# Order tables of a fused cross-attention and sparse-FFN kernel: gather a step later, two products in halves, the first scores ahead of the first values

## The chip, the cores and the metric

One NeuronCore of one Trainium2 chip runs the whole program in one launch. The number looked at is the device time of one execution in microseconds (us). Before the change it is 963.16 us, the median of three runs between 959.63 and 963.48 us.

## What is computed

Eight batches of 512 queries by 256 features attend to 1024 context rows with 16 heads of 16 features; then a router picks 128 of the 512 rows of each batch, these go through causal self-attention and a gated FFN, and are put back:

```
q, k, v = LN(x) @ Wq.T, ctx @ Wk.T, ctx @ Wv.T          # 16 heads of 16
x = x + softmax(q k.T / 4, masked keys off) v @ Wo.T
y = LN(x)
idx = top_k(y @ w_router, 128);  x_sel = y[idx]          # the 128 best rows
h = rmsnorm(x_sel, g1);  att = causal_attention(h @ Wqkv.T) @ Wout.T
h2 = rmsnorm(x_sel + att, g2)
x_ff = silu(h2 @ W1.T) * (h2 @ W2.T) @ W3.T              # 682 wide
out = x + y, with idx rows replaced: x[idx] + x_sel + att + x_ff
```

All data are float32. The weights' layout is prepared on the host.

## The kernel before, in words

The program is written engine by engine: each of TensorE (PE), VectorE (DVE), ScalarE (ACT), GpSimd (POOL) and SyncE (SP, which issues the DMAs) has its list of instructions, in an order written out by hand, and they meet in semaphores. Nothing is scheduled by a planner.

After a prologue, an outer loop goes over the eight batches, here called passes 0 to 7, and each pass has 32 steps: 4 head groups by 8 key tiles of 128. In step s, PE issues

- the *scores* of step s (`pe_scores`, L436): four products of 32x128 keys by 32x512 queries into two of three PSUM bank pairs, once ACT has freed both. ACT turns them into `probs` with two Exp instructions of 128x1024 (L466), each of which frees its pair;
- the *values* of step s-1 (`pe_values`, L455): `probs` by `va` into `o_bank`, once ACT's second Exp of that step is done. At the first tile of a head group (steps 1, 9, 17, 25, where s-1 is a multiple of 8) they wait for `o_free` too: `dve_norm` (L544, stages norm0 to norm3) has to have read the group before out of `o_bank`;
- a *filler*: one stage of other work, as the table `PE_SLOT` says, with the step as its number. All fillers of the loop write one PSUM bank, `m_bank` (`MISC`), and take it when ACT or DVE has evicted the filler before (`take_bank`, `bank_free`).

A step with no filler is called empty below. The fillers are of two kinds. "P" is projection for the next batch: keys `K00` to `K11`, values `V0` to `V3`, the transposes `xT0`, `xT1` of the normalised input, queries `Q0`, `Q1`. "F" is the output projection and the FFN of the batch before: `wo0`, `wo1`, `spread` (router scores onto all partitions), then on DVE `rank0` to `rank3`, which end in the selection matrix `sel`, then `gather` (`sel` by `y`), `selT`, `hidT`, `kq`, `v`, `fs` (FFN attention scores), `pv`, `wout`, `hid2T`, `u0`, `w0`, `u1`, `w1`, `down` (the last product, by W3), `scat1`, `scat0`. Pass 0 has no "F" and, in the table `PE_SLOT_0`, the rest of batch 0's own projections ("I"); pass 7 has no "P". `ACT_SLOT` and `DVE_ORDER` say in which order ACT and DVE evict.

In the prologue PE runs 18 products of no use (`spare_products`, L257), then K00, the transposes, K01 and Q0 of batch 0; then it transposes the table of valid keys (`valid`, L988), which DVE copies, and computes V0, which DVE multiplies by it. Only then does the loop begin. After pass 7 a tail runs the FFN of batch 7 with nothing beside it but more products of no use.

Of the kernel before, what the change touches and what calls it, by code (L numbers as in the profile page):

```python
# [5 lines left out]
P = 128  # L6
# [3 lines left out]
D = 256  # L10
# [4 lines left out]
KC = D // P  # L15
# [12 lines left out]
FT = 6  # L28
# [14 lines left out]
MISC = 7  # L43

BANK_FIRST = {"xT0": 0, "xT1": 1, "K00": 2, "Q0": 3, "K01": 4, "valid": 5, "V0": 7}
# [11 lines left out]
           ("F", "fs", FS_STEP, False), ("P", "Q0", 16, False), ("P", "V2", 17, False), ("P", "Q1", 18, False),  # L57
# [3 lines left out]
ACT_SLOT = [("P", "K00", 0), ("P", "K01", 1), ("P", "K10", 5), ("F", "spread", 6), ("P", "K11", 7), ("P", "xT0", 8),  # L61
            ("P", "xT1", 9), ("F", "selT", 11), ("F", "hidT", 12), ("F", "v", 15), ("F", "fs", FS_STEP), ("P", "differ", 21),
            ("F", "hid2T", 23), ("F", "u0", 24), ("F", "u1", 26)]
DVE_ORDER = [("A", "norm3"), ("F", "wo0"), ("F", "wo1"), ("P", "V0"), ("F", "y"), ("P", "stats"), ("P", "xn"), ("F", "rank0"),
# [4 lines left out]

PE_SLOT_0 = [("I", "V1", 0, False), ("I", "K10", 1, False), ("I", "V2", 2, False), ("I", "K11", 3, False),  # L70
# [4 lines left out]
ACT_SLOT_0 = [("I", "K10", 1), ("I", "K11", 3), ("P", "K00", 8), ("P", "K01", 9), ("P", "K10", 10), ("P", "K11", 11),  # L75
              ("P", "xT0", 15), ("P", "xT1", 17), ("P", "differ", 20)]
DVE_ORDER_0 = [("I", "V1"), ("I", "V2"), ("I", "V3"), ("I", "Q1"), ("P", "stats"), ("N", "norm0"), ("P", "xn"), ("P", "V0"),
# [12 lines left out]
SPARE_FIRST = 18  # L90

# [8 lines left out]
def program(nc, io, out):  # L100
    with ExitStack() as top:
# [163 lines left out]
        def pe_project(pe, stage, i):  # L265
# [32 lines left out]
        def pe_ffn(pe, stage, i):  # L298
# [73 lines left out]
            elif stage == "down":  # L372
                pe.wait_ge(gate_ready, 2)
                pe.sem_inc(gate_ready, -2)
                dst = take_bank(pe, i)
                product(dst[:, 0:D], [(gate[:, f], w3[:, f]) for f in range(FT)]).then_inc(done["down"], 1)
# [412 lines left out]
        with ExitStack() as ctx:  # L789
# [129 lines left out]
            def _(dve):  # L919
# [19 lines left out]
                dve_project(dve, "V0", 0, BANK_FIRST["V0"], valid[:, 0])  # L939
# [42 lines left out]
            def _(pe):  # L982
                def valid_keys():
                    pe.wait_ge(consts, 1)
# [343 lines left out]
```

## Time and profile before

| | |
|---|---|
| median of 3 runs | 963.16 us (959.63 to 963.48) |
| profiled execution, its time | 963.8 us |
| its span, first to last instruction | 962.0 us |
| granted TensorE clock, mean | 0.993 |
| PE busy | 896.8 us (93%) |
| ACT busy | 575.0 us (60%) |
| DVE busy | 340.8 us (35%) |
| POOL busy | 79.0 us (8%) |
| 16 DMA engines | 34 GB/s on average |

In the chain of time the passes look like this in the trace: the first scores start at 23.78 us, pass 1 at about 124 us, pass 3 runs from 345.09 to 456.84 us, pass 7 from 789.90 us, and the tail from about 888 us to the end. The busy time of an engine counts an instruction from start to modelled end; where two overlap they count once. A time is read below mostly from start to start: between the start of one group and that of the next lies all that the first costs, its wait for the next included.

### The profile page before, as it was taken

What the parts mean: (1) busy time and instruction counts of PE and PEld (TensorE: products, weight loads), DVE (VectorE), ACT (ScalarE), POOL (GpSimd) and SP (SyncE); (2) the same over time, 40 slices, a digit from 0 to 9 for tenths busy, and PEclk for the clock granted to TensorE, in tenths of its full rate; (3) what the DMA queues carried; (4) which work ended last, traced back from release to release, by engine and by line L of the source; (5) the groups of instructions that cost most, each with busy time, mean ns of one, the idle gap of its engine ahead of it and who ended that gap; (6) DMA issues with size and microseconds to landing.
All of it is one profiled execution on the core that took longest, in us unless ns stands there. A gap on an engine that the chain in (4) does not pass through costs nothing. (4 is left out here: it accounts for less than half of the span.)

```text
span 962.0 us, 25188 instructions
## 1 busy us (share of the span) xinstructions
PE 896.8 (93%) x10277; PEld 338.6 (35%) x10277; DVE 340.8 (35%) x886; ACT 575.0 (60%) x653; POOL 79.0 (8%) x130
## 2 busy tenths in 40 slices
PE   6999999999999999999999999999989999899874
PEld 2323232333333432334323433334323332334434
DVE  2222136232543227331453316342273315321631
ACT  2567766666666666665576766666666767676010
POOL 4000100010100101000000101011001100010010
PEclk9999999999999999999999999999999999999998
DMA  5150200020010200020010200002000000000000
GB/s 170 42 184 1 72 3 23 24 73 24 5 42 2 73 23 23 23 68 15 16 39 8 73 23 24 24 3 72 24 1 24 29 24 1 24 2 24 1 1 25
DMA packets 23789, 32.47 MB, mean 34 GB/s; under 512 B 1102, under 2 KB 20856, under 8 KB 23672
## 3 DMA queue, kind: packets, MB, share of 16 engines
q1 hardware_dynamic: 23672, 30.81, 9.9%
q8 instruction: 85, 1.39, 0.6%
q14 instruction: 32, 0.26, 0.1%
HBM read 26.61 MB, written 4.19 MB: 32 GB/s over the span
## 5 line engine op out<-in xcount | busy, mean ns | idle before, releaser
L466 ACT ACTIVATE probs<-pair_bank 128x1024 f32<-128x1024 f32 x512 | 496.3, 1021 | 270.6 <-ACTq L465 270.6
L436 PE MATMUL pair_bank<-q_sb,k_sb 32*128 32x512 f32 x2048 | 292.1, 639 | 13.9 <-PEq L434 13.9
L455 PE MATMUL o_bank<-probs,va 128*32 128x512 f32 x2048 | 272.7, 604 | 6.3 <-PEq L449 5.2
L436 PEld LDWEIGHTS pair_bank<-q_sb,k_sb 32*128 32x128 f32 x2048 | 81.3, 183 | 140.0 <-issue 140.0
L455 PEld LDWEIGHTS o_bank<-probs,va 128*32 128x32 f32 x2048 | 41.3, 108 | 197.2 <-issue 110.9
L252 PE MATMUL m_bank<-wv_sb,ctx_in 128*32 128x256 f32 x1024 | 62.8, 386 | 0.6 <-PEq L262 0.6
L544 DVE STREAM_TRANSPOSE o_blk<-o_bank 128x512 f32<-128x512 f32 x32 | 22.9, 717 | 110.5 <-DVEq L543 110.5
L252 PE MATMUL m_bank<-ctx_in,wk_sb 128*32 128x512 f32 x480 | 57.0, 592 | 0.0
L585 DVE TENSOR_SCALAR va<-m_bank,valid 128x256 f32<-128x256 f32 x64 | 28.0, 479 | 80.8 <-DVEq L579 80.8
L252 PEld LDWEIGHTS m_bank<-hid_t,w 128*32 128x32 f32 x1440 | 41.3, 111 | 19.5 <-issue 19.4
L252 PE MATMUL m_bank<-hid_t,w 128*32 128x128 f32 x1440 | 46.0, 275 | 2.2 <-PEq L262 1.7
L252 PEld LDWEIGHTS m_bank<-wv_sb,ctx_in 128*32 128x32 f32 x1024 | 33.8, 111 | 36.7 <-issue 21.1
L597 DVE TENSOR_SCALAR q_sb<-m_bank,parity 128x512 f32<-128x512 f32 x30 | 21.1, 747 | 34.3 <-DVEq L595 34.3
L474 ACT ACTIVATE k_sb<-m_bank 128x512 f32<-128x512 f32 x30 | 17.9, 597 | 24.2 <-ACTq L473 24.2
L614 DVE TENSOR_TENSOR x<-x,m_bank 128x512 f32<-128x512 f32 x14 | 9.6, 688 | 61.7 <-DVEq L613 61.7
L257 PE MATMUL o_bank<-before 128*128 128x512 bf16 x118 | 28.8, 402 | 2.7 <-POOL before L846 2.7
L754 POOL TENSOR_TENSOR mask_in<-mask_in,mask_row 128x256 int32<-128x256 int32 x32 | 23.3, 760 | 78.8 <-POOLq L751 78.8
L252 PE MATMUL m_bank<-xn_t,wq_sb 128*32 128x512 f32 x240 | 28.6, 595 | 0.0
L252 PEld LDWEIGHTS m_bank<-ctx_in,wk_sb 128*32 128x32 f32 x480 | 15.6, 110 | 35.9 <-issue 35.9
L769 POOL TENSOR_SCALAR_AFFINE_SELECT p_f<-p_f 128x2048 f32<-128x2048 f32 x8 | 16.1, 2006 | 141.9 <-POOLq L767 141.9
L762 POOL TENSOR_SCALAR veps<-mv 128x4 f32<-128x4 f32 x8 | 1.9, 233 | 311.0 <-POOLq L761 311.0
L252 PE MATMUL m_bank<-wo,o_t 128*32 128x256 f32 x448 | 26.7, 379 | 0.0
(168 smaller groups left out, 647.0 us busy)
## 6 DMA issues: line engine op xcount, KB each, us to landing
ctx_in<-in_ctxT SPq DMA_DIRECT2D x8, 1024.0 KB, 7.3
x_in<-in_x SPq DMA_DIRECT2D x8, 512.0 KB, 3.9
x<-in_x SPq DMA_DIRECT2D x8, 512.0 KB, 3.7
mask_in<-in_mask SPq DMA_DIRECT2D x8, 512.0 KB, 3.9
out_dram<-out_sb SPq DMA_DIRECT2D x8, 512.0 KB, 2.8
mask_row<-in_mask SPq DMA_DIRECT2D x8, 128.0 KB, 5.4
wqkv<-in_wqkvT SPq DMA_DIRECT2D x1, 768.0 KB
w<-in_w1T SPq DMA_DIRECT2D x1, 682.0 KB
```

What stands on the lines that cost most here:

```text
L252: last = nc.tensor.matmul(dst[j], a[:, j], c, start=(n == 0), stop=(n == len(pairs) - 1))
L257: last = nc.tensor.matmul(dst, before[:, 0, 0:P], before[:, 1], start=True, stop=True)
L436: last = nc.tensor.matmul(pair_bank[pairs[r // 2]][:, r % 2], key_tile(b, s, r), query_tile(b, s, r), start=True, stop=True)
L455: last = nc.tensor.matmul(o_bank[32 * r:32 * r + 32], va[b % 2][:, t, HV * h:HV * h + 32], probs[s % 2][:, r], start=(t == 0), stop=(t == ...
L466: nc.scalar.activation(probs[s % 2][:, 2 * e:2 * e + 2, :], pair_bank[p][:], ACT.Exp, scale=HD ** -0.5).then_inc(s_free[p], 1)
L474: nc.scalar.activation(k_sb[b % 2][:, m, half * 512:(half + 1) * 512], bank[i], ACT.Copy).then_inc(bank_free[i], 1)
L544: nc.vector.transpose(o_blk[:], o_bank[:]).then_inc(o_free, 1)
L585: last = nc.vector.tensor_scalar(by_head(va[b % 2][:, t])[:, :, 0:HD], bank[i][:, e * D:(e + 1) * D].rearrange("p (h d) -> p h d", h=H), o ...
L597: last = nc.vector.tensor_scalar(q_sb[b % 2][:, m, par], bank[i], parity[:, par:par + 1], None, ALU.mult)
L614: nc.vector.tensor_tensor(x1[:, 2 * pr:2 * pr + 2], x1[:, 2 * pr:2 * pr + 2], bank[i].rearrange("p (t d) -> p t d", t=2), ALU.add).then_in ...
L754: last = nc.gpsimd.tensor_tensor(mask_words[:, t * WORDS:(t + 1) * WORDS], mask_words[:, t * WORDS:(t + 1) * WORDS], first, ALU.subtract)
L769: nc.gpsimd.affine_select(out=flat, in_=flat, compare_op=ALU.is_ge, fill=0.0, base=0, pattern=[[0, H], [1, CAP]], channel_multiplier=-1).t ...
```

## The change

It is one edit of tables, with what they need:

- `gather` and its followers `selT`, `hidT` go from steps 10, 11, 12 to 11, 12, 13; `kq` and what comes later stay. `V1`, which stood at step 13, goes to 17, `V2` from 17 to 18, `Q1` from 18 to 20, `V3` from 20 to the empty step 22.
- `K11`, the fourth piece of keys, is computed in two halves (`K11:0`, `K11:1`) in steps 7 and 8; `xT0`, `xT1` go from 8, 9 to 9, 10.
- `down` is computed in two halves in steps 28 and 29; `scat1`, `scat0` go from 29, 30 to 30, 31. Step 31 was empty.
- Batch 0's `valid` and `V0` leave the prologue for step 0 of pass 0, after scores(0), and use `m_bank`; the other "I" stages go one step later. In their place 10 products of no use stand after Q0, and the semaphore `spare_done`, which GpSimd waits for before it finishes the constant `before`, moves behind them.

A half of a product takes the bank only in its first part and signals only after its second. The tail keeps `down` whole.

```diff
-           ("P", "V0", 4, True), ("P", "K10", 5, False), ("F", "spread", 6, False), ("P", "K11", 7, False),
-           ("P", "xT0", 8, False), ("P", "xT1", 9, False), ("F", "gather", 10, False), ("F", "selT", 11, False),
...
+           ("P", "V0", 4, True), ("P", "K10", 5, False), ("F", "spread", 6, False), ("P", "K11:0", 7, False), ("P", "K11:1", 8, False),
+           ("P", "xT0", 9, False), ("P", "xT1", 10, False), ("F", "gather", 11, False), ("F", "selT", 12, False),
...
-             ("F", "rank1"), ("N", "norm0"), ("F", "rank2"), ("F", "rank3"), ("F", "gather"), ("F", "base"), ("P", "V1"),
-             ("F", "kq"), ("N", "norm1"), ("P", "Q0"), ("P", "V2"), ("P", "Q1"), ("F", "pv"), ("P", "V3"), ("F", "wout"),
+             ("F", "rank1"), ("N", "norm0"), ("F", "rank2"), ("F", "rank3"), ("F", "gather"), ("F", "base"),
+             ("F", "kq"), ("N", "norm1"), ("P", "Q0"), ("P", "V1"), ("P", "V2"), ("F", "pv"), ("P", "Q1"), ("F", "wout"),
...
+        def share(part, n):
+
+            return range(n) if part is None else range(part * n // 2, (part + 1) * n // 2)
...
-                dst = take_bank(pe, i)
-                product(dst, [(wk[:, c, m * P:(m + 1) * P], ctx_in[:, c, half * 512:(half + 1) * 512]) for c in range(KC)]
-                        ).then_inc(done["K"], 1)
+                dst = bank[i] if part == 1 else take_bank(pe, i)
+                last = product(dst, [(wk[:, c, m * P:(m + 1) * P], ctx_in[:, c, half * 512:(half + 1) * 512])
+                                     for c in share(part, KC)], part != 1, part != 0)
+                if part != 0:
+                    last.then_inc(done["K"], 1)
...
-                spare_products(SPARE_FIRST, o_bank[:]).then_inc(spare_done, 1)
+                spare_products(SPARE_FIRST, o_bank[:])
...
-                valid_keys()
-                pe.wait_ge(w_in["wv"], 16)
-                pe_project(pe, "V0", BANK_FIRST["V0"])
+                spare_products(SPARE_Q0, o_bank[:]).then_inc(spare_done, 1)
```

The next two blocks are PE's order in pass 2 from `spread` (step 6) to `selT`, before and then after; L436 and L449 are the scores, L455 and L468 the values.

```order
204 L243 MATMUL m_bank<-ident,score 128x128 x4
205 L436 MATMUL pair_bank<-q_sb,k_sb 128x512 x4
206 L455 MATMUL o_bank<-probs,va 32x512 x4
207 L252 MATMUL m_bank<-ctx_in,wk_sb 32x512 x8
208 L436 MATMUL pair_bank<-q_sb,k_sb 128x512 x4
209 L455 MATMUL o_bank<-probs,va 32x512 x4
210 L243 MATMUL m_bank<-ident,xn 128x128 x4
...
216 L252 MATMUL m_bank<-y,sel 32x256 x16
```

```order
207 L245 MATMUL m_bank<-ident,score 128x128 x4
208 L449 MATMUL pair_bank<-q_sb,k_sb 128x512 x4
209 L468 MATMUL o_bank<-probs,va 32x512 x4
210 L254 MATMUL m_bank<-ctx_in,wk_sb 32x512 x4
211 L449 MATMUL pair_bank<-q_sb,k_sb 128x512 x4
212 L468 MATMUL o_bank<-probs,va 32x512 x4
213 L254 MATMUL m_bank<-ctx_in,wk_sb 32x512 x4
214 L449 MATMUL pair_bank<-q_sb,k_sb 128x512 x4
215 L468 MATMUL o_bank<-probs,va 32x512 x4
216 L245 MATMUL m_bank<-ident,xn 128x128 x4
...
222 L254 MATMUL m_bank<-y,sel 32x256 x16
```

Between `spread` and the gather (`y,sel`) there are now five pairs of scores and values instead of four, and the same filler work; half of the keys' product lies one step later. In the last steps of the same pass, `down` and what follows it on PE stood and stand so:

```order
270 L252 MATMUL m_bank<-w,gate 32x256 x24
271 L436 MATMUL pair_bank<-q_sb,k_sb 128x512 x4
272 L455 MATMUL o_bank<-probs,va 32x512 x4
273 L252 MATMUL m_bank<-att,sel_t 32x256 x8
...
276 L252 MATMUL m_bank<-att,sel_t 32x256 x8
277 L436 MATMUL pair_bank<-q_sb,k_sb 128x512 x4
278 L455 MATMUL o_bank<-probs,va 32x512 x4
279 L436 MATMUL pair_bank<-q_sb,k_sb 128x512 x4
```

```order
274 L254 MATMUL m_bank<-w,gate 32x256 x12
275 L449 MATMUL pair_bank<-q_sb,k_sb 128x512 x4
276 L468 MATMUL o_bank<-probs,va 32x512 x4
277 L254 MATMUL m_bank<-w,gate 32x256 x12
...
283 L254 MATMUL m_bank<-att,sel_t 32x256 x8
284 L449 MATMUL pair_bank<-q_sb,k_sb 128x512 x4
285 L468 MATMUL o_bank<-probs,va 32x512 x4
286 L254 MATMUL m_bank<-ctx_in,wk_sb 32x512 x8
```

Two values followed by scores with nothing between them (rows 278, 279) are the empty step 31; it is now filled. At the program's start PE's order was and is:

```order
5 L252 MATMUL pair_bank<-xn_t,wq_sb 32x512 x8
6 L988 MATMUL pair_bank<-ident,rows 128x64
7 L252 MATMUL m_bank<-wv_sb,ctx_in 32x256 x16
8 L436 MATMUL pair_bank<-q_sb,k_sb 128x512 x4
9 L252 MATMUL m_bank<-wv_sb,ctx_in 32x256 x16
```

```order
5 L254 MATMUL pair_bank<-xn_t,wq_sb 32x512 x8
6 L264 MATMUL o_bank<-before 128x512 x10
7 L449 MATMUL pair_bank<-q_sb,k_sb 128x512 x4
8 L1003 MATMUL m_bank<-ident,rows 128x64
9 L254 MATMUL m_bank<-wv_sb,ctx_in 32x256 x16
10 L449 MATMUL pair_bank<-q_sb,k_sb 128x512 x4
```

The first scores now stand ahead of the transpose of the valid keys (`rows`) and of V0 (`wv_sb,ctx_in`).

## Rows read from the trace of the kernel before

**Rows 1.** Windows: length; busy us (instructions) of PE, PEld, DVE, ACT, POOL; clock; DMA.

```profile
20.00:40.00 20.00, 19.16 (x197) 6.98 (x201) 3.50 (x16) 8.95 (x10) 0.63 (x1) 0.91 0.01 2
345.09:456.84 111.75, 107.43 (x1268) 40.27 (x1269) 42.42 (x109) 71.34 (x82) 9.03 (x13) 1.00 0.10 31
```

**Rows 2.** Waits of PE: us in total, times, longest.

```profile
PE pair_bank L436 <- PEq L434: 13.9, 40, 1.3
```

**Rows 3.** Timeline of pass 3, PE, steps 7 to 10: start, us, instructions [idle before].

```profile
372.44 1.90 PE L252 MATMUL m_bank<-ctx_in,wk_sb 128*32 128x512 f32 x16
374.27 1.14 PE L436 MATMUL pair_bank<-q_sb,k_sb 32*128 32x512 f32 x8
...
376.93 1.14 PE L436 MATMUL pair_bank<-q_sb,k_sb 32*128 32x512 f32 x8
378.85 1.06 PE L455 MATMUL o_bank<-probs,va 128*32 128x512 f32 x8 [0.79 <-PEq L449]
...
381.50 1.06 PE L455 MATMUL o_bank<-probs,va 128*32 128x512 f32 x8
383.98 1.93 PE L252 MATMUL m_bank<-y,sel 128*32 128x256 f32 x32 [1.41 <-PEq L262]
```

**Rows 4.** The same stretch, DVE: norm0's first read, and the last `sel`.

```profile
378.03 0.72 DVE L544 STREAM_TRANSPOSE o_blk<-o_bank 128x512 f32<-128x512 f32 x1 [0.19 <-DVEq L543]
...
383.36 0.29 DVE L647 TENSOR_SCALAR sel<-iota_r,rank 128x128 f32<-128x128 f32 x1
```

**Rows 5.** Timeline of pass 3, PE, steps 20 to 23.

```profile
419.30 1.91 PE L252 MATMUL m_bank<-wv_sb,ctx_in 128*32 128x256 f32 x32
421.14 1.14 PE L436 MATMUL pair_bank<-q_sb,k_sb 32*128 32x512 f32 x8
422.21 1.06 PE L455 MATMUL o_bank<-probs,va 128*32 128x512 f32 x8
423.10 1.05 PE L252 MATMUL m_bank<-wout,os_t 128*32 128x256 f32 x16
424.07 1.14 PE L436 MATMUL pair_bank<-q_sb,k_sb 32*128 32x512 f32 x8
...
426.74 1.14 PE L436 MATMUL pair_bank<-q_sb,k_sb 32*128 32x512 f32 x8 [0.53 <-PEq L434]
```

**Rows 6.** Timeline, PE: scores of pass 3's step 31 and of pass 4's step 0.

```profile
454.41 1.14 PE L436 MATMUL pair_bank<-q_sb,k_sb 32*128 32x512 f32 x8
...
456.84 1.14 PE L436 MATMUL pair_bank<-q_sb,k_sb 32*128 32x512 f32 x8 [0.30 <-PEq L434]
```

**Rows 7.** Timeline, PE: pass 7, scores of step 10 and its gather.

```profile
817.46 1.14 PE L436 MATMUL pair_bank<-q_sb,k_sb 32*128 32x512 f32 x8 [0.24 <-PEq L434]
821.27 1.93 PE L252 MATMUL m_bank<-y,sel 128*32 128x256 f32 x32 [1.68 <-PEq L262]
```

**Rows 8.** Timeline of the start: Q0 and its eviction, valid keys, V0, first scores.

```profile
15.62 1.90 PE L252 MATMUL pair_bank<-xn_t,wq_sb 128*32 128x512 f32 x16
...
17.70 1.41 DVE L597 TENSOR_SCALAR q_sb<-pair_bank,parity 128x512 f32<-128x512 f32 x2 [5.97 <-DVEq L595]
...
20.28 0.24 PE L988 MATMUL pair_bank<-ident,rows 64*128 64x64 f32 x1 [2.77 <-PEq L262]
...
20.45 3.39 PE L252 MATMUL m_bank<-wv_sb,ctx_in 128*32 128x256 f32 x32
20.56 0.23 DVE L936 COPY valid<-pair_bank 128x64 f32<-128x64 f32 x1 [0.53 <-PE pair_bank L988]
...
23.78 1.31 PE L436 MATMUL pair_bank<-q_sb,k_sb 32*128 32x512 f32 x8
```

**Rows 9.** Timeline, PE: V1 after the eviction of V0; scores(8) of pass 0.

```profile
25.65 1.93 PE L252 MATMUL m_bank<-wv_sb,ctx_in 128*32 128x256 f32 x32 [0.56 <-PEq L262]
...
51.31 1.14 PE L436 MATMUL pair_bank<-q_sb,k_sb 32*128 32x512 f32 x8 [0.29 <-PEq L434]
```

**Rows 10.** Timeline, PE: twelve products of no use at the tail's start.

```profile
888.83 2.76 PE L257 MATMUL pair_bank<-before 128*128 128x512 bf16 x12
```

More of the change, by code:

```diff
@@ L43 @@
 MISC = 7
-BANK_FIRST = {"xT0": 0, "xT1": 1, "K00": 2, "Q0": 3, "K01": 4, "valid": 5, "V0": 7}
+BANK_FIRST = {"xT0": 0, "xT1": 1, "K00": 2, "Q0": 3, "K01": 4, "valid": MISC}
 BANK_LAST = {"wo0": 0, "wo1": 1, "spread": 7, "gather": 0, "selT": 1, "hidT": 7, "kq": 0, "v": 1, "pv": 7, "wout": 0,
@@ L53 @@
 PE_SLOT = [("P", "K00", 0, False), ("P", "K01", 1, False), ("F", "wo0", 2, False), ("F", "wo1", 3, False),
[3 rows of a table removed]
-           ("F", "fs", FS_STEP, False), ("P", "Q0", 16, False), ("P", "V2", 17, False), ("P", "Q1", 18, False),
[1 row of a table removed]
[3 rows of a table added]
+           ("F", "fs", FS_STEP, False), ("P", "Q0", 16, False), ("P", "V1", 17, False), ("P", "V2", 18, False),
+           ("F", "pv", 19, False), ("P", "Q1", 20, False), ("F", "wout", 21, False), ("P", "V3", 22, False),
+           ("F", "hid2T", 23, False),
            ("F", "u0", 24, False), ("F", "w0", 25, False), ("F", "u1", 26, False), ("F", "w1", 27, False),
[1 row of a table removed]
-ACT_SLOT = [("P", "K00", 0), ("P", "K01", 1), ("P", "K10", 5), ("F", "spread", 6), ("P", "K11", 7), ("P", "xT0", 8),
-            ("P", "xT1", 9), ("F", "selT", 11), ("F", "hidT", 12), ("F", "v", 15), ("F", "fs", FS_STEP), ("P", "differ", 21),
+           ("F", "down:0", 28, False), ("F", "down:1", 29, False), ("F", "scat1", 30, False), ("F", "scat0", 31, False)]
+ACT_SLOT = [("P", "K00", 0), ("P", "K01", 1), ("P", "K10", 5), ("F", "spread", 6), ("P", "K11", 8), ("P", "xT0", 9),
+            ("P", "xT1", 10), ("F", "selT", 12), ("F", "hidT", 13), ("F", "v", 15), ("F", "fs", FS_STEP), ("P", "differ", 21),
             ("F", "hid2T", 23), ("F", "u0", 24), ("F", "u1", 26)]
 DVE_ORDER = [("A", "norm3"), ("F", "wo0"), ("F", "wo1"), ("P", "V0"), ("F", "y"), ("P", "stats"), ("P", "xn"), ("F", "rank0"),
[3 rows of a table removed]
[3 rows of a table added]
              ("F", "scat0")]
-PE_SLOT_0 = [("I", "V1", 0, False), ("I", "K10", 1, False), ("I", "V2", 2, False), ("I", "K11", 3, False),
[1 row of a table removed]
+PE_SLOT_0 = [("I", "valid", 0, False), ("I", "V0", 0, False), ("I", "V1", 1, False), ("I", "K10", 2, False),
[1 row of a table added]
              ("P", "K10", 10, False), ("P", "K11", 11, False), ("P", "V0", 12, False), ("P", "V1", 13, False),
@@ L74 @@
              ("P", "V3", 21, False), ("P", "Q1", 23, False)]
-ACT_SLOT_0 = [("I", "K10", 1), ("I", "K11", 3), ("P", "K00", 8), ("P", "K01", 9), ("P", "K10", 10), ("P", "K11", 11),
+ACT_SLOT_0 = [("I", "K10", 2), ("I", "K11", 4), ("P", "K00", 8), ("P", "K01", 9), ("P", "K10", 10), ("P", "K11", 11),
               ("P", "xT0", 15), ("P", "xT1", 17), ("P", "differ", 20)]
-DVE_ORDER_0 = [("I", "V1"), ("I", "V2"), ("I", "V3"), ("I", "Q1"), ("P", "stats"), ("N", "norm0"), ("P", "xn"), ("P", "V0"),
+DVE_ORDER_0 = [("I", "V0"), ("I", "V1"), ("I", "V2"), ("I", "V3"), ("I", "Q1"), ("P", "stats"), ("N", "norm0"), ("P", "xn"), ("P", "V0"),
                ("P", "V1"), ("N", "norm1"), ("P", "V2"), ("P", "Q0"), ("P", "V3"), ("P", "Q1"), ("N", "norm2")]
@@ L246, in program, with product @@
         strips = [slice(j, j + 32) for j in range(0, P, 32)]
-        def product(dst, pairs):
+        def product(dst, pairs, begins=True, ends=True):
             for n, (a, c) in enumerate(pairs):
                 for j in strips:
-                    last = nc.tensor.matmul(dst[j], a[:, j], c, start=(n == 0), stop=(n == len(pairs) - 1))
-            return last
+                    last = nc.tensor.matmul(dst[j], a[:, j], c, start=(begins and n == 0),
+                                            stop=(ends and n == len(pairs) - 1))
+            return last
+        def share(part, n):
+            return range(n) if part is None else range(part * n // 2, (part + 1) * n // 2)
         def spare_products(n, dst):
@@ L372, in pe_ffn @@
             elif stage == "down":
[L373 to L376, printed above, removed]
+                if part != 1:
+                    pe.wait_ge(gate_ready, 2)
+                    pe.sem_inc(gate_ready, -2)
+                dst = bank[i] if part == 1 else take_bank(pe, i)
+                last = product(dst[:, 0:D], [(gate[:, f], w3[:, f]) for f in share(part, FT)], part != 1, part != 0)
+                if part != 0:
+                    last.then_inc(done["down"], 1)
             elif stage in ("scat1", "scat0"):
@@ L1020, in _ @@
                         for stage, at, early, kind in todo:
-                            if at == s and not early and kind in ("P", "I"):
-                                pe_project(pe, stage, MISC)
+                            if at == s and stage == "valid":
+                                valid_keys()
+                            elif at == s and not early and kind in ("P", "I"):
+                                pe_project(pe, *stage_part(stage))
                             elif at == s and not early and stage == "fs":
```

16 lines of the change are left out of this document (9 added, 7 removed), and 8 rows, old and new, of tables (DVE_ORDER, PE_SLOT, PE_SLOT_0).

## The prediction, made before the changed kernel was run

> **What bounds the kernel now.** I read the window of a middle pass first [rows 1]: in pass 3 PE is busy 107.43 of 111.75 us, at a granted clock of 1.00, ACT 71.34 and DVE 42.42. The reader is to see that PE's list of products sets the time, so that the change, which removes no product, can only win where PE waits, some 4 us a pass. Then the waits of PE [rows 2] name the commonest one: scores that wait for ACT (L434), 40 times, 13.9 us. Last the timeline of PE in one pass for the places, with DVE beside it for what ends them [rows 3 to 6].
>
> I count from start to start. In a step whose filler is full size, scores take 1.07 us (421.14 to 422.21) and values 0.89 (422.21 to 423.10) [rows 5], 1.95 together, and the filler's own time comes on top. An empty step should take 1.95 and takes 2.43 (454.41 to 456.84) [rows 6], because the next scores need a pair of banks that ACT has still to read. So an empty step wastes 0.48 us, and any filler over that size hides ACT.
>
> **Gather a step later, keys in halves.** Before, values(9) start at 381.50 and the gather could start 0.89 later, at 382.39; it starts at 383.98, 1.59 later [rows 3], since the last `sel` ends at 383.65 [rows 4]. There is a second wait above it: scores(9) start at 376.93, values(8) could start 1.07 later, at 378.00, and start at 378.85, 0.85 later [rows 3]. These values open a head group and need `o_bank` read by norm0, whose transpose runs from 378.03 to 378.75 [rows 4]; it stands on DVE behind rank1. DVE's chain up to norm0 starts from `spread` in step 6, ahead of everything moved, so I take 378.85 as fixed.
>
> A half product costs more than half. A filler of 16 instructions (wout) takes 0.97 (423.10 to 424.07), one of 32 of the same shape (V3) 1.84 (419.30 to 421.14) [rows 5]: two small ones are 0.10 more than one large one, the price of a boundary. K11 takes 1.83 (372.44 to 374.27) [rows 3], a half so 0.97. After the change: K11:0 at 372.44, scores(8) 373.41, K11:1 at 375.36, scores(9) 376.33, values(8) wanted at 377.40. They wait for norm0 until 378.85, 1.45 us: 0.60 more than before, with the boundary hidden in the wait. From there the times are as before through scores(10) at 380.43 and values(9) at 381.50; then xT1 (0.69, as xT0 has it between values(8) and scores(10): 380.43 - 378.85 - 0.89) instead of the gather, scores(11) at 383.08, the gather at 385.03. `sel` has been ready for 1.4 us. So 1.59 goes, 0.60 comes back at norm0 and 0.10 of work is added: **0.9 us a pass**. What is late next is norm0; the cover of the gather is 1.4 us.
>
> `hidT` and `kq` now stand in neighbouring steps. `hid` follows the gather through DVE and POOL as before and moves with it, so `hidT` waits for nothing new. `kq` waits for ACT's eviction of `hidT`, with 1.95 us of scores and values between; I take nothing. V1, V2 and Q1 only change places; K11's eviction moves with its second half, and POOL's list is the same in the loop.
>
> **Step 22.** It was empty and followed a step in which ACT also squares the mask: scores(22) at 424.07, scores(23) at 426.74 [rows 5], 2.67 for 1.95. With V3 there, **0.7 us a pass** go. V3's eviction comes two steps later, hence `ctx_free`, on which SP queues the next context load, a store behind it. The context is wanted at step 0 of the next pass, ten steps of some 3.5 us later: hidden. The store and the loads behind it in SP's queue slip a step at most and are needed steps later.
>
> **Step 31.** `down` in halves and scat1, scat0 a step later fill it: 0.48 less 0.10 for the boundary, **0.38 a pass**, in pass 7 too.
>
> **Pass 7** has no "P". Scores(10) start at 817.46, the gather at 821.27 [rows 7]: 3.81 for 1.95, so 1.86 waits. After, step 10 is empty in place of step 13, at 2.43 both, and the gather, at 821.84, comes 0.9 after the `sel` that it waited for. With step 31 2.24.
>
> **The start.** Q0 ends about 17.46, DVE evicts it until 19.11; PE idles to 20.28, transposes the valid keys, and V0 takes 3.33 until the scores at 23.78 [rows 8], where V1 costs 1.93 busy [rows 9]; the granted clock of that stretch is 0.91 against 1.00 [rows 1]. V0, right behind the idle time, ran at the lower of the two levels (1.2 GHz), and that cost 1.5 us. After: ten products of no use, 0.23 each at full clock (2.76 for 12 [rows 10]), to 19.76, past Q0's eviction; scores(0) 19.76, valid at 20.83. V0 now shares `m_bank` with it and waits for DVE's copy: 0.51 from transpose to end of the copy [rows 8], and 0.3 for the way back, the gap between `sel` and the gather [rows 3, 4]. V0 21.64, scores(1) 23.48. Values(0) wait for V0's eviction: V1 waited for it before, from V0's end at 23.78 to 25.65, 1.87 [rows 8, 9]. So values(0) at 25.35, 0.8 late, V1 at 26.24, scores(2) 28.08, then five full steps (K10, V2, K11, V3, Q1) of 3.79 and the empty step 7: scores(8) at 49.5 against 51.31 [rows 9]. **1.8 us**, net of the added products.
>
> On that clock there is a rule in the Trainium skill (TensorE: Matmul & The Clock Gate, Part 1: The HAM clock gate): the array runs at half rate by default and is released by activity, and idling throttles it again. The trace agrees where PE idled 2.77 us ahead of V0 and V0 took 3.39. By that rule the ten products keep the clock up. The page also says (Part 2, single matmul latency) that a lone product cannot hide its drain while a stream can, which speaks against halves: an estimate from its 166 ns at the high clock would charge 13 added boundaries 2.2 us. The 0.10 of the rows decides, of which seven count, 0.7 us.
>
> **Sum.** Six passes (1 to 6) at 0.9 + 0.72 + 0.38 = 2.0 are 12.0; pass 7 2.2; the start 1.8: 16.0 us. The tail is untouched. The profiled execution took 963.8 us with 1.8 outside its span; it stands 0.6 above the median. So 947.8 on its own scale, about **947 us** on the median's.
>
> **Bounds of what the trace does not show.** The start: if the ten products and the first steps run at the low level, they take twice 0.23 each and V0 3.33, which costs 3.8 and turns 1.8 into -2.0; if values(0) wait for nothing, it is +2.6. I take 1.8, nearest to the rows at full clock. Gather: between 0.3 (the 1.59 taken back by norm0 and by `kq` behind `hidT`) and 1.5 (norm0 no later relative to the values); 0.9 is worked from a time that I hold fixed. A boundary: from nothing to twice 0.10; step 22: 0.5 to 0.7. Together a gain of 6 x 1.1 + 1.5 - 2.0 = 6 us at the low end and 6 x 2.7 + 2.4 + 2.6 = 21 at the high end, 957 and 942. Passes also differ by up to 1 us with the same work; these need not stay.
>
> **Rivals.**
> 1. *The start gives nothing back.* The clock falls in spite of the ten products, or V0, now between scores and values, delays both. For: two new waits within 5 us of the loop's begin (0.8 for the bank, 0.8 for V0's eviction). Against: each is shorter than the 2.77 that came before the low clock. Start at -2.0: 950.8 us.
> 2. *The gather's wait moves rather than goes.* Norm0 stands in DVE's list between rank1 and rank2 and PE now comes to values(8) sooner. If the wait there takes all that the gather's gave up, 5.4 us are missing: 952.4 us. For: 0.85 us of it is there already. Against: norm0's start hangs on DVE's chain, which PE's order after `spread` doesn't touch.
> 3. *One bank for all fillers becomes the bound*, and the time is higher than before. With every step filled, each filler waits for the eviction of the one before, with 1.95 us of cover. Q0's eviction ends 1.65 after its product and 0.2 to 0.3 more brings the bank back [rows 8]; Q1 now stands ahead of wout, and `hidT` ahead of `kq`. Cover is nearly used up for Q1. To be slower by 0.5%, 20.8 us must be lost at the 13 such places (seven times `hidT` to `kq`, six times Q1 to wout), 1.6 us each; at 1.7 us the time is 969 us. Against: in the trace Q1 stands in step 18 ahead of pv, and pv shows no wait.
> 4. *The change doesn't do what it says*: the freed steps meet stalls of another kind (DVE or ACT late for one step), and only the empty steps 22 and 31 give, 7 us: 956 us.
>
> **How the numbers follow.** My forecast has 0.60, rival 1 0.17, rival 2 0.13, rival 4 0.06, rival 3 0.04. What a measurement can tell from no change is 0.5%, 4.8 us, so faster is below 958.3. Forecast and rivals 1 and 2 are faster, rival 4 mostly (0.04 of 0.06): 0.94 faster, 0.02 within, 0.04 slower. The range, 942.5 to 954 us, takes in the forecast's own and rivals 1 and 2.
>
> **What would show it.** Right: in passes 1 to 6 no wait ahead of the gather, 1.4 to 1.5 us ahead of values(8), no empty step from 0 to 31, a pass in 108.6 to 109.5 us; scores(0) near 19.8 us, V0 in about 1.9 us, scores(8) of pass 0 near 49.5; pass 7 without a wait at its gather. Wrong: a wait at the gather or at `kq`, one at wout behind Q1's eviction, V0 at 3.3 us, or halves that cost more than 0.97 and 1.41 us.

## The result and the profile after

The changed kernel takes 946.38 us, the median of four runs (944.77 to 948.13), against 962.21 us (959.63 to 963.48, four runs) for the kernel before beside it: a ratio of 0.984, 95% interval 0.981 to 0.987. A second series gave 946.38 us again (0.984, 0.982 to 0.985). That is 15.8 us; the forecast was 16.0, 947 us. So close a match is luck: the start was off by 3.0 us one way, and passes 1 to 6 by 2.1 and the tail, whose code the change leaves alone, by 0.6 the other way. The experiments are mostly about the first two.

The profiled execution took 947.94 us with a span of 946.2, against 963.8 and 962.0. Cut at scores(0) of passes 1 and 7 and at the tail's first product of no use, the two traces compare so:

| stretch | before, us | after, us | gained | forecast |
|---|---|---|---|---|
| start to scores(0) of pass 1 | 123.62 | 124.86 | -1.24 | 1.8 |
| passes 1 to 6 | 666.28 | 652.14 | 14.14 | 12.0 |
| pass 7 | 98.93 | 96.60 | 2.33 | 2.2 |
| tail, to the end of the span | 73.17 | 72.6 | 0.6 | 0 |

This is PE in pass 3 of the changed kernel, steps 7 to 11, from the timeline (start, us, instructions, idle before); L449 are the scores, L468 the values, and it answers to [rows 3].

```profile
369.28 1.04 PE L254 MATMUL m_bank<-ctx_in,wk_sb 128*32 128x512 f32 x8
370.25 1.14 PE L449 MATMUL pair_bank<-q_sb,k_sb 32*128 32x512 f32 x8
...
372.21 1.04 PE L254 MATMUL m_bank<-ctx_in,wk_sb 128*32 128x512 f32 x8
373.18 1.14 PE L449 MATMUL pair_bank<-q_sb,k_sb 32*128 32x512 f32 x8
376.03 1.07 PE L468 MATMUL o_bank<-probs,va 128*32 128x512 f32 x8 [1.71 <-issue]
...
381.33 1.06 PE L468 MATMUL o_bank<-probs,va 128*32 128x512 f32 x8
382.22 1.91 PE L254 MATMUL m_bank<-y,sel 128*32 128x256 f32 x32
```

And DVE beside it, answering to [rows 4]: norm0's transpose and the last `sel`.

```profile
375.21 0.72 DVE L557 STREAM_TRANSPOSE o_blk<-o_bank 128x512 f32<-128x512 f32 x1 [0.54 <-DVEq L556]
...
380.53 0.29 DVE L660 TENSOR_SCALAR sel<-iota_r,rank 128x128 f32<-128x128 f32 x1
```

A half product takes 0.97 (369.28 to 370.25), as forecast. The gather follows its values after 0.89 with no wait, 1.4 us after `sel` (380.82). The wait sits ahead of values(8) now, and ends with norm0's transpose (375.93). The profile calls its cause "issue", but the time fits DVE's end to 0.1 us. Here it is 1.71, in passes 5 and 6 1.62 and 1.68; in passes 1, 2 and 4 it is 1.37. Why norm0 comes later in three of the passes no run shows. Step 22 and the end of the pass, answering to [rows 5, 6]:

```profile
418.50 1.14 PE L449 MATMUL pair_bank<-q_sb,k_sb 32*128 32x512 f32 x8
...
420.45 1.91 PE L254 MATMUL m_bank<-wv_sb,ctx_in 128*32 128x256 f32 x32
422.29 1.14 PE L449 MATMUL pair_bank<-q_sb,k_sb 32*128 32x512 f32 x8
...
440.18 1.48 PE L254 MATMUL m_bank<-w,gate 128*32 128x256 f32 x24
441.59 1.14 PE L449 MATMUL pair_bank<-q_sb,k_sb 32*128 32x512 f32 x8
```

V3 ends where the next scores start, without a wait, and half of `down` takes 1.41. The window of the whole pass, with the columns of [rows 1]:

```profile
341.94:450.81 108.87, 106.86 (x1272) 40.19 (x1268) 41.91 (x109) 71.29 (x82) 8.85 (x13) 1.00 0.10 32
```

Pass 3 went from 111.75 to 108.87 us, PE's busy time hardly: what went is idle time. The start is another matter. PE, DVE and POOL there, answering to [rows 8, 9] (L264 are the products of no use):

```profile
17.70 2.11 PE L264 MATMUL o_bank<-before 128*128 128x512 bf16 x9 [0.16 <-issue]
...
19.90 1.14 PE L449 MATMUL pair_bank<-q_sb,k_sb 32*128 32x512 f32 x8
...
21.65 1.93 PE L254 MATMUL m_bank<-wv_sb,ctx_in 128*32 128x256 f32 x32 [0.41 <-PEq L269]
...
22.73 2.79 POOL L767 TENSOR_TENSOR mask_in<-mask_in,mask_row 128x256 int32<-128x256 int32 x4 [0.28 <-POOLq L764]
23.51 1.14 PE L449 MATMUL pair_bank<-q_sb,k_sb 32*128 32x512 f32 x8
23.75 2.04 DVE L595 COPY va<-valid 128x16 f32<-128x16 f32 x8 [2.25 <-DVEq L592]
...
25.70 0.86 DVE L598 TENSOR_SCALAR va<-m_bank,valid 128x256 f32<-128x256 f32 x2
26.76 1.55 PE L468 MATMUL o_bank<-probs,va 128*32 128x512 f32 x8 [2.11 <-PEq L465]
28.01 3.23 PE L254 MATMUL m_bank<-wv_sb,ctx_in 128*32 128x256 f32 x32
31.17 1.14 PE L449 MATMUL pair_bank<-q_sb,k_sb 32*128 32x512 f32 x8
```

Up to scores(1) all is as worked out: scores(0) 19.90 (19.76), V0 21.65 (21.64) at the full clock, scores(1) 23.51 (23.48). Then the eight copies of the valid column take DVE 2.04 us, not 0.7, values(0) start at 26.76 instead of 25.35, and behind 2.11 us without work the clock is at its lower level: V1 takes 3.23. The granted clock says the same (0.91 over the window below; 0.50 of 2.4 GHz in the part from 28 to 30 us, 1.00 from 32 us on):

```profile
20.00:40.00 20.00, 17.48 (x181) 7.01 (x185) 4.79 (x15) 8.35 (x9) 5.24 (x9) 0.91 0.01 2
```

Scores(2) were forecast for 28.08 and start at 31.17, 3.1 later, and that is the whole miss of the start: scores(8) at 52.55 against 49.5 forecast.

### The profile page after: what moved, and what is told of

Its sections match the earlier page's. It is cut to its first block and busy times, and to the rows that moved or that the text cites. A ratio compares the mean times of both kernels' runs of the same rounds, so it can differ in the third digit from the quotient of the medians.

```text
span 946.2 us, 25202 instructions
## 1 busy us (share of the span) xinstructions
PE 895.5 (95%) x10280; PEld 338.3 (36%) x10287; DVE 339.9 (36%) x886; ACT 574.7 (61%) x653; POOL 78.1 (8%) x130
## 3 DMA queue, kind: packets, MB, share of 16 engines
q8 instruction: 85, 1.39, 0.6%
## 5 line engine op out<-in xcount | busy, mean ns | idle before, releaser
L449 PE MATMUL pair_bank<-q_sb,k_sb 32*128 32x512 f32 x2048 | 292.1, 639 | 8.8 <-PEq L447 8.7
L468 PE MATMUL o_bank<-probs,va 128*32 128x512 f32 x2048 | 273.2, 605 | 11.5 <-issue 9.1
L449 PEld LDWEIGHTS pair_bank<-q_sb,k_sb 32*128 32x128 f32 x2048 | 81.0, 183 | 131.1 <-issue 131.1
L468 PEld LDWEIGHTS o_bank<-probs,va 128*32 128x32 f32 x2048 | 41.3, 108 | 202.0 <-issue 117.7
L264 PE MATMUL o_bank<-before 128*128 128x512 bf16 x122 | 31.4, 413 | 3.3 <-POOL before L859 2.7
L653 DVE SCALAR_TENSOR_TENSOR ties<-all_scores,score,before 128x512 f32<-128x512 f32 x32 | 24.1, 752 | 6.6 <-DVEq L652 4.8
```

The costliest lines, as they stand in the source:

```text
L264: last = nc.tensor.matmul(dst, before[:, 0, 0:P], before[:, 1], start=True, stop=True)
L449: last = nc.tensor.matmul(pair_bank[pairs[r // 2]][:, r % 2], key_tile(b, s, r), query_tile(b, s, r), start=True, stop=True)
L468: last = nc.tensor.matmul(o_bank[32 * r:32 * r + 32], va[b % 2][:, t, HV * h:HV * h + 32], probs[s % 2][:, r], start=(t == 0), stop=(t == ...
L653: nc.vector.scalar_tensor_tensor(out=ties[t % 2][:], in0=all_scores[:], scalar=score[:, t:t + 1], in1=before[:, t], op0=ALU.is_equal, op1= ...
```

## The experiments

All start from the changed kernel but e11. Times are medians, each with its ratio to the kernel before beside it. "Scores(8)" is their start in pass 0 in the profiled execution; in the changed kernel it is 52.55 us, in the kernel before 51.31. The runs come from several series, and the median of the kernel before moved between 960.8 and 962.4 us from one to the next; a difference of medians from different series is good to about 1.5 us, and the stretches of the traces tell more.

| kernel | us | ratio (95%) | scores(8) |
|---|---|---|---|
| changed, two series | 946.38, 946.38 | 0.984 (0.981 to 0.987), 0.984 (0.982 to 0.985) | 52.55, 52.57 |
| e1, old start | 944.4 | 0.983 (0.981 to 0.985) | 50.32 |
| e2, own tile | 943.95 | 0.981 (0.980 to 0.983) | 49.70 |
| e3, copies first | 944.02 | 0.981 (0.980 to 0.983) | 48.82 |
| e4, gap filled | 945.82 | 0.984 (0.981 to 0.986) | 50.97 |
| e10, e2 without the ten | 946.81 | 0.984 (0.982 to 0.987) | 50.83 |
| e5, K11 whole | 946.63 | 0.985 (0.983 to 0.987) | |
| e6, norm0 first | 942.07 | 0.981 (0.979 to 0.983) | |
| e7, down whole | 948.88 | 0.988 (0.986 to 0.989) | |
| e8, old middle | 956.27 | 0.996 (0.994 to 0.997) | |
| e9, e2 + e3 + e6 | 939.77 | 0.976 (0.974 to 0.978) | |
| e11, before, mask sooner | 959.5 | 0.997 (0.995 to 0.999) | |

**e1, the start as before.**

```diff
-                spare_products(SPARE_Q0, o_bank[:]).then_inc(spare_done, 1)
+                valid_keys()
+                pe_project(pe, "V0", BANK_FIRST["V0"])
```

(with `PE_SLOT_0`, `ACT_SLOT_0`, `DVE_ORDER_0`, the banks and `spare_done` as in the kernel before)

> The changed kernel with the start of the kernel before: valid keys and V0 in the prologue, no ten products, the other stages of batch 0 a step earlier again. The traces put scores(8) of pass 0 at 51.31 us before and at 52.55 after, so my theory now is that the new start costs 1.2 us: this kernel is 1.2 us faster than the profiled execution of the changed one, about 946.7 on the profiled scale (947.9 there), with the passes unchanged at 108.4 to 108.9 us. The rival, my prediction's own sum, says that the new start is worth 1.8 us and its loss was a disturbance of one execution: then this kernel takes 1.8 us more than an undisturbed run of the changed one (944.8), 946.6, and scores(8) lies at 51.3 in both cases. What tells them apart is the changed kernel's other runs, two at 944.8 and two at 948: the start may be worth 1.8 in some and cost 1.2 in others.

Measured: 944.4 us, scores(8) at 50.32. The new start costs time, 2.2 us between the two traces and about 2 between the medians, though those intervals overlap. It is more than the expected 1.2, because in this execution the old start itself was quicker than in the kernel before: PE waited 2.21 us for the valid keys, not 2.77, and V0 took 2.95, not 3.39. The first has a cause in the traces: DVE's conversion of the valid keys' table (`rows`), ahead of PE's transpose, began at 19.25 in both and took 0.23 instead of 0.78, with GpSimd's mask differences beside it in both. The prediction's 1.8 us of gain is refuted.

**e2, GpSimd as early as before.** The ten products read a tile of their own, and `spare_done` stands again behind the first 18.

```diff
+        spare = sb("spare", [P, S], BF16)
...
-                spare_products(SPARE_FIRST, o_bank[:])
+                spare_products(SPARE_FIRST, o_bank[:]).then_inc(spare_done, 1)
...
-                spare_products(SPARE_Q0, o_bank[:]).then_inc(spare_done, 1)
+                own_spares(SPARE_Q0, o_bank[:])
```

> The changed kernel, but the ten products after Q0 read a tile of their own, so spare_done is signalled after the first 18 products as in the kernel before and GpSimd finishes `before` and does batch 0's mask differences (L767) some 4.9 us earlier. Theory (GpSimd in DVE's way): the eight copies of the valid column ahead of V0's eviction took 2.04 us instead of 0.74 because GpSimd's mask differences ran beside them (22.73 to 25.5 us); moved to about 17.9 to 20.6 us they are gone: copies 0.7, values(0) at 25.4 instead of 26.76, the clock stays at the high level, V1 takes 1.93 instead of 3.23, scores(8) of pass 0 at 49.5, every run near 943.5 to 944.5. Rival (the copies were slow for another reason, such as reading `valid` just written): copies still 2.0 us, scores(8) at 52.5 in a run with the low clock, runs at 944.8 to 948.

Measured: 943.95 us, and the timeline of its start:

```profile
17.89 2.77 POOL L773 TENSOR_TENSOR mask_in<-mask_in,mask_row 128x256 int32<-128x256 int32 x4 [3.73 <-POOLq L770]
...
23.92 0.72 DVE L601 COPY va<-valid 128x16 f32<-128x16 f32 x8 [2.25 <-DVEq L598]
...
25.60 1.06 PE L474 MATMUL o_bank<-probs,va 128*32 128x512 f32 x8 [0.78 <-PEq L471]
26.46 1.94 PE L255 MATMUL m_bank<-wv_sb,ctx_in 128*32 128x256 f32 x32
```

DVE's list is the same; only GpSimd's place in time is another, and the copies take 0.72 instead of 2.04. Values(0) wait 0.78, as the prediction had it (0.8), and no product of the start runs at the low level. The theory holds, its numbers too (49.70 against 49.5). The page SBUF — State Buffer of the Trainium skill says (its term "shared port pair") that VectorE and GpSimd arbitrate for one pair of ports with an exclusive lock; these two traces agree in that the copies take longer beside GpSimd, 2.04 against 0.72 us. DVE's eviction from PSUM, begun at 25.70 when GpSimd ended (25.52), took its usual 0.86, so they say nothing of evictions beside GpSimd.

**e3, copies ahead of the wait.**

```diff
-                dve.wait_ge(done["V"], 1)
-                dve.sem_inc(done["V"], -1)
+                if n == 0 and b == 0:
+                    copies()
+                dve.wait_ge(done["V"], 1)
+                dve.sem_inc(done["V"], -1)
```

> The changed kernel, but for batch 0 DVE makes the eight copies of the valid column before it waits for V0 instead of after. If the chain from V0 to values(0) is what stalls PE, the copies run from about 21.6 us beside V0, before GpSimd's mask differences begin at 22.7, and V0's eviction is 0.87 us from 23.8: values(0) at about 24.8 instead of 26.76, no low clock, scores(8) of pass 0 at about 48.9 us, runs at 943 to 944. If GpSimd still comes in DVE's way, the eviction waits for it to end (25.5) and values(0) stay near 26.7.

Measured: 944.02 us, values(0) at 24.73, scores(8) at 48.82, the earliest of all. The copies, begun at 21.55, were slow again, 1.87 us, with GpSimd at `before` until 22.1 and at the mask from 22.63, but PE no longer waited for them. One detail is against my expectation of a blocked eviction: it ran from 23.66 to 24.54 beside GpSimd's mask differences in 0.88, its usual time. In this execution what reads PSUM was not held up; the copies within SBUF were.

**e4, the wait filled with work of no use.**

```diff
+                        if b == 0 and s == 1:
+                            own_spares(8, o_bank[:])
```

> The changed kernel with eight more products of no use (0.23 us each) in the wait ahead of values(0), step 1 of pass 0, on a tile of their own. It takes the low clock apart from the wait: theory (the 2.11 us of idle PE let the clock fall, and the low level cost 1.7 us): values(0) still at about 26.8, but V1 1.93 instead of 3.23 and values(0) 1.07 instead of 1.55, scores(8) of pass 0 at 50.9 instead of 52.55, runs at 946.3 or less and less spread than 944.8 to 948.1. Rival (the clock falls whatever PE does there): V1 at 3.2 us again, scores(8) at 52.5.

```profile
24.71 1.90 PE L270 MATMUL o_bank<-spare 128*128 128x512 bf16 x8
...
26.87 1.07 PE L474 MATMUL o_bank<-probs,va 128*32 128x512 f32 x8 [0.27 <-PEq L471]
27.73 1.94 PE L255 MATMUL m_bank<-wv_sb,ctx_in 128*32 128x256 f32 x32
```

Values(0) come as late (26.87), yet V1 takes 1.94, scores(2) follow values(0) after 2.73 us instead of 4.41, and scores(8) start 1.6 us sooner. So of the 3.1 us missed at the start 1.4 are the copies and 1.7 the clock behind the wait. In the medians this is within the noise (945.82 against 946.38), and the runs spread as before, 944.63 to 948.95. The runs of this program differ for another reason too: the two profiled executions of the changed kernel, 1.56 us apart, both have the low clock there (V1 at 3.23 and 3.60) and scores(8) at 52.55 and 52.57; they part in the tail, 72.6 against 71.1 us. The low clock came in five of the six profiled executions that had this 2.1 us wait; in e8's it did not, with nothing else changed in pass 0.

**e10, e2 without the ten products.** The line `own_spares(SPARE_Q0, o_bank[:])` is gone.

> The kernel with the ten products on their own tile (943.95 us), without those ten products; GpSimd is as early as there. Theory (the ten products are there for the clock): PE idles some 1.9 us behind Q0, scores(0) start about 0.5 us sooner, at 19.4, and the clock may fall behind it: V0 or V1 at 3 us as in the old start, 1.0 to 1.5 us lost, 944.5 to 945. Rival (an idle stretch under 2 us doesn't bring the low clock): no product at the low level, scores(8) of pass 0 at 49.2, 943.5 us, and the ten products are worth nothing.

```profile
19.84 1.14 PE L455 MATMUL pair_bank<-q_sb,k_sb 32*128 32x512 f32 x8 [2.36 <-PEq L453]
...
21.68 3.19 PE L255 MATMUL m_bank<-wv_sb,ctx_in 128*32 128x256 f32 x32 [0.41 <-PEq L275]
```

V0 runs at the low level. Scores(0) win nothing, against the 0.5 us expected: here as in e2 they start 4.26 us after Q0 does (Q0 itself is 0.23 sooner), so the ten products cost no time. Scores(8) are 1.13 us later than in e2 (1.36 counted from Q0), which is what those products are worth here. The median is 2.9 us higher; of the 2.1 us between the two profiled executions another 1.3 lies in pass 7, whose code is the same (97.68 against 96.37 us), where the low level came behind a wait of 1.28 us ahead of scores(17) in e10 and not in e2. The Trainium skill's rule that the prediction cited (TensorE: Matmul & The Clock Gate, Part 1: The HAM clock gate) fits e2, e4 and e10: idle ahead, low level behind. It does not tell e8 from the five others.

**e5, K11 whole in step 7, step 8 empty.**

```diff
-("P", "K11:0", 7, False), ("P", "K11:1", 8, False),
+("P", "K11", 7, False),
```

> The changed kernel with K11 whole in step 7 and step 8 empty; all else as changed. By the prediction's working values(8) wait for norm0 at a time that PE doesn't move, so the halves gain nothing there: the empty step's 0.48 us is taken out of the wait, which shrinks from 1.4 to about 1.1 us, a pass stays at 108.4 to 108.9 us and the time within 0.5 us of the changed kernel. Rival (a filled step is worth its 0.48 here too, less 0.10 for the boundary): 0.38 a pass, 2.3 us slower.

Measured: 946.63 us, passes 1 to 6 in 652.80 us against 652.14, 0.1 a pass. The wait ahead of values(8) fell from 1.37 to 1.00. The halves of K11 gain next to nothing: norm0 sets the time at that place.

**e6, norm0 ahead of rank1 on DVE.**

```diff
-             ("F", "rank1"), ("N", "norm0"), ("F", "rank2"), ...
+             ("N", "norm0"), ("F", "rank1"), ("F", "rank2"), ...
```

> The changed kernel with norm0 ahead of rank1 in DVE's order. Theory: the 1.4 to 1.7 us that values(8) wait in each of the six passes end because norm0's transpose starts about 2 us sooner, right behind rank0; the last sel stays where it is, and so the gather, 1.4 us ahead of its need until now, would wait about 0.1 to 0.4 us. A gain of 1.0 to 1.4 us a pass, 6 to 8 us in all. Rival (PE has no use for the earlier values since the next link, the end of the rank chain, is as late): the wait moves to the gather in full and nothing is gained.

Values(8) and the gather of pass 3 in its timeline:

```profile
372.25 1.06 PE L468 MATMUL o_bank<-probs,va 128*32 128x512 f32 x8
...
378.81 1.93 PE L254 MATMUL m_bank<-y,sel 128*32 128x256 f32 x32 [0.18 <-PEq L269]
```

942.07 us; passes 1 to 6 take 645.56 us, 6.6 less or 1.10 a pass, and the gather waits 0.18 to 0.49 there. Pass 7 pays: its gather waits 0.87, which it did not before, and the pass takes 1.06 us more, 97.66. The expectation had 6 to 8 us in all and left that out; the traces say 5.5 for the seven passes, the medians 4.3. What the change left at values(8) was real idle time, and one swap collects most of it.

**e7, down whole in step 28.**

```diff
-("F", "down:0", 28, False), ("F", "down:1", 29, False), ("F", "scat1", 30, False), ("F", "scat0", 31, False)]
+("F", "down", 28, False), ("F", "scat1", 29, False), ("F", "scat0", 30, False)]
```

> The changed kernel with down whole in step 28, the scatters in 29 and 30, step 31 empty again. Theory: seven passes pay 0.48 for the empty step and save 0.10 for the boundary: 0.38 each, 2.7 us slower than the changed kernel. Rival (halves cost more than 0.10, up to what a drained pipeline would cost, 0.17 each, or hide something else): between 1.5 and 4 us slower.

948.88 us, 2.5 slower; passes 1 to 6 take 654.37 us, 0.37 a pass more, and pass 7 0.84. A boundary is 0.1 us, not the 0.17 of the rival.

**e8, the middle of a pass as before.**

```diff
-("P", "K11:0", 7, False), ("P", "K11:1", 8, False), ("P", "xT0", 9, False), ("P", "xT1", 10, False), ("F", "gather", 11, False), ...
+("P", "K11", 7, False), ("P", "xT0", 8, False), ("P", "xT1", 9, False), ("F", "gather", 10, False), ..., ("P", "V1", 13, False), ...
```

> The changed kernel with the middle of a pass as before: K11 whole in step 7, the transposes in 8 and 9, gather, selT, hidT in 10, 11, 12, V1 in 13; V2 in 17, Q1 in 20, V3 in 22, and step 18 empty. Theory: in passes 1 to 6 the wait at the gather is back (1.6 from start to start for 0.6 less at norm0, 0.1 less for the boundary) and step 18 wastes 0.48: 1.4 us a pass, 8.3 in six, and 1.9 in pass 7: 10.2 us slower than the changed kernel. Rival (the gather's place is worth little, the gain came from passes that had stalls in the kernel before): only the 0.48 of step 18 in six passes and little more, 3 us.

956.27 us, 9.9 slower. Passes 1 to 6 take 660.90 us, 8.8 more (8.3 expected), pass 7 98.46, 1.9 more. The waits are back to the digit in passes 1 and 2: 0.78 ahead of values(8) and 1.40 at the gather; the others have up to 0.35 more at one of the two. The gather's place, with the step that it fills, is well over half of the whole gain; the two are not taken apart, and the empty step (18 here) is 0.48 a pass of it by the sum.

**e9, three edits together.** e2, e3 and e6.

> The changed kernel with three of the edits tried before together: norm0 ahead of rank1, the ten products on a tile of their own (so GpSimd works as early as in the kernel before), the eight copies for batch 0 ahead of the wait for V0. If the edits add up: 942.07 of norm0 first, less the 2.4 us by which either start edit beat the changed kernel, less up to 0.8 us because values(0) wait for nothing: 939 to 940 us. Rival (the start edits and norm0 first share a gain, or the time won at the start is lost again in pass 0, which has empty steps): no better than 941.

939.77 us, a ratio of 0.976 to the kernel before (0.974 to 0.978), the fastest of all. Its 6.6 us against the changed kernel are what the parts promise.

**e11, the kernel before with the mask squared in step 20.** One entry of `ACT_SLOT`:

```diff
-("F", "fs", FS_STEP), ("P", "differ", 21),
+("F", "fs", FS_STEP), ("P", "differ", 20),
```

> The kernel before (not the changed one) with one entry changed: ACT squares the mask (`differ`) in step 20 instead of 21, so the next mask is loaded and GpSimd takes its differences (L754) one step, 3.8 us, sooner. The passes gained 2.1 us more than the prediction's sum, and in the kernel before GpSimd's differences overlap norm2's multiplication on DVE (L549) in passes 2 to 5, where that took 0.68 to 0.99 us instead of 0.42, and w0 waited up to 1.0 us; in the changed kernel they don't overlap. Theory (that collision is the 2.1 us): all L549 at 0.42, no wait at w0 in passes 1 to 6, 2.0 us gained; and as ACT now squares beside a full step, the wait ahead of scores(23) falls from 0.53 to 0.30, 1.4 us more: 3.4 us faster than the kernel before. Rival (the waits at w0 have another cause): they stay, and only the 1.4 us are gained.

To read it, first pass 3 of the kernel before, timeline of POOL, DVE and PE in steps 24 and 25 (L754 are the mask differences, L549 norm2's multiplication, L252 at 435.69 is w0):

```profile
431.85 2.98 POOL L754 TENSOR_TENSOR mask_in<-mask_in,mask_row 128x256 int32<-128x256 int32 x4 [4.95 <-POOLq L751]
...
432.62 0.93 DVE L549 TENSOR_TENSOR o_nrm<-o_blk,inv_all 128x256 f32<-128x256 f32 x1
...
435.69 1.52 PE L252 MATMUL m_bank<-hid_t,w 128*32 128x128 f32 x48 [1.00 <-PEq L262]
```

The same place in the changed kernel, DVE:

```profile
428.18 0.43 DVE L562 TENSOR_TENSOR o_nrm<-o_blk,inv_all 128x256 f32<-128x256 f32 x1
```

And in e11, POOL:

```profile
427.12 2.79 POOL L754 TENSOR_TENSOR mask_in<-mask_in,mask_row 128x256 int32<-128x256 int32 x4 [1.17 <-POOLq L751]
```

with L549 at 431.44 in 0.43 us. In e11 no pass has a wait at w0, all L549 take 0.42 or 0.43, and scores(23) wait 0.30 instead of 0.53. 959.5 us against 962.38 is a gain of 2.9 (1.3 to 4.8 by the interval), 3.4 expected; the interval takes in the rival's 1.4 too. In its trace passes 1 to 6 take 662.42 us (785.98 less 123.56) against 666.28, so 3.9 less: 1.4 is the 0.23 at scores(23) in each pass, and 2.45 lies in step 25, that of w0, in passes 2, 3 and 5 alone (0.39, 1.21, 0.85). That is the place of the 2.1 us that the passes gained beyond the sum.

What held PE there is less clear than the expectation has it, and more rows of the kernel before speak against L549 as the cause. They are DVE's eviction of u0 in pass 3 and PE's w0 in pass 5:

```profile
433.75 0.55 DVE L704 SCALAR_TENSOR_TENSOR silu<-half_tanh,m_bank 128x384 f32<-128x384 f32 x1 [0.19 <-DVEq L703]
...
657.12 1.04 PE L252 MATMUL m_bank<-hid_t,w 128*32 128x128 f32 x26
658.61 0.86 PE L252 MATMUL m_bank<-hid_t,w 128*32 128x128 f32 x22 [0.45 <-issue]
```

In pass 3 the bank that w0 takes was evicted at 434.30, and w0 began 1.39 us later. In pass 5 w0 began without a wait and broke off for 0.45 after 26 of its 48 products. Only in pass 2 does w0 (323.94) follow the eviction (323.80) closely. Nor does a long L549 bring a wait: 0.68 in pass 4 brought none, nor did 0.90 in pass 2 of e8, and the second profiled execution of the changed kernel has 0.66, 0.65 and 0.57 in passes 2 to 4 with the passes as long as in the first. A break like that of pass 5 (0.78 us at 926.38) stands in the tail of the changed kernel, with GpSimd at rest. So e11 shows that the waits go when the mask's squaring, its load and GpSimd's differences come a step sooner; which of these, or something else such as the supply of PE's instructions, held PE is open.

**The changed kernel again.**

> The changed kernel once more, to see what its spread is made of. Two of its runs took 944.8 us and two 948. Theory (the low clock behind the 2.1 us wait ahead of values(0) comes in some executions and not in others): runs again in two groups about 2 to 3 us apart, the lower with a mean granted clock of 0.997, the higher 0.991 to 0.994. Rival: evenly spread, with no tie to the clock.

946.38, 946.67, 948.08, 946.02 and 944.84 us: no two groups. The lowest has the highest granted clock (0.997), the highest the lowest (0.993), but the three between don't part. My theory of two groups falls; both profiled executions of this kernel have the low clock in pass 0, so no run shows that it makes this spread; what the two differ by lies in the tail.

## Why the prediction was right

The total was right, 15.8 us for 16.0, by luck in that the start's miss and the surplus elsewhere cancelled. The mechanism of the loop, which is nine tenths of the forecast, was right by its own measurements. By its steps:

- **Gather, 0.9 us a pass:** right. The wait is gone, values(8) come 1.44 us late from start to start in undisturbed passes (1.45 forecast), and e8, which undoes it and leaves one more step empty, costs 8.8 us where 1.4 a pass, 8.3, were worked out from the same terms. The prediction charged the halves of K11 as part of the edit; e5 shows that they are not what gains.
- **Step 22, 0.7, and step 31, 0.38:** right. Scores(22) to scores(23) is 3.79 us, a full step and nothing more; e11 shows that 0.23 of the 0.72 was the wait beside ACT's squaring. e7 measures the second at 0.37. With the first term they make 2.0 a pass, and the shortest pass went from 110.56 to 108.54 us, 2.02.
- **Pass 7, 2.2:** measured 2.33, closer than it can claim: with the same code pass 7 takes 96.19 to 97.68 us in eight profiled executions (both of the changed kernel, e1 to e5 and e10).
- **A boundary, 0.10, hidden once:** right, by 0.97 and 1.41 us for the halves.
- **The start, 1.8:** wrong, and the step of it that failed is "Values(0) wait for V0's eviction: V1 waited for it before ... 1.87". That 1.87 was measured with GpSimd at rest. The front names that `spare_done` moves behind the ten products, and rival 1 spoke of two new waits, but neither asked what GpSimd does when it is let go 8 us later: its mask differences moved from 17.87 to 22.73 us, onto DVE's copies. e2 takes that away and returns 2.85 us of scores(8): with it the sum's 49.5 is met (49.70). The low level of the clock, which the prediction expected to be gone, came back one product later (e4). Rival 1, the start at -2.0, is thus what happened to the start: -1.24, with the passes' surplus over it.
- **Passes 1 to 6 at 12.0:** 2.1 too small. The prediction said of the extra time in some passes that it "need not stay", without a cause. It had a place, visible in the trace: step 25 of passes 2, 3 and 5, where w0 starts late or breaks off. e11 makes it go; what held PE there stays open.
- Rival 2 (the wait moves to values(8)) held for 0.9 of 5.4 us: from start to start values(8) come 9.55 us late in the six passes, for 8.7 charged; rival 3 (one bank) did not show: no wait at `kq` or wout in any pass.

## What to carry to other kernels

When every product is needed, list the steps with no filler and the waits with their releasers, and price a move from start to start: that gave 2.0 us for an undisturbed pass, and 2.02 was measured. An edit that moves a semaphore moves the whole queue behind it; ask which engine it lets go later, and what that engine then runs beside, GpSimd beside DVE above all. When two engines run side by side where a third waits, look whether the wait ends with either of them before calling the overlap its cause. A wait removed or made at PE is worth more than its length if the clock falls behind it, and a few products of no use in the gap are cheap cover.

## What the runs showed of the hardware

- Eight copies of 128x16 within SBUF on DVE take 0.72 us with GpSimd idle (six executions) and 1.87 to 2.04 beside its work (eight); a multiplication of 128x256 with both inputs in SBUF 0.42 and 0.57 to 0.99. An eviction from PSUM takes 0.87 alone and 0.88 in e3, beside GpSimd. It is not so each time: the conversion of `rows` (64x128), 0.22 otherwise, took 0.78, 0.67, 0.62 and 0.38 beside GpSimd's mask differences in the kernel before, e10, e2 and e11, and 0.23 in e1.
- An idle stretch of PE of 2.1 to 2.8 us at the start was followed by products at 1.2 GHz, which cost 1.0 to 1.7 us, in nine of ten profiled executions: the kernel before (2.77), e1 (2.21), e10 (2.36), e11 (2.36, with V0 at 3.45), and five of the six with the 2.1 us wait. With 0.8 us or less there (e2, e3, e9), or with the gap filled (e4), it was not.
- Length alone does not tell: pass 7 has a wait of 1.28 us ahead of scores(17) in every execution, and the lower level came behind it in three of fourteen (e3, e9, e10), at 1.2 to 1.3 us each; behind the 1.36 to 1.73 us ahead of values(8) in passes 1 to 6 it never came.
